# ViT tower on one NeuronCore: GpSimd adds the exponentials of attention 1's two key tiles, one row-sum product per head, one patch buffer, a new table of steps

## The reference

```
h = cat(cls, LN(LN(patches) @ W + b))
# attention 1
q, k, v = split((LN(h)) @ w_qkv.T)          # 12 heads x 64
q, k = q * rsqrt(norm(q over heads)), k * rsqrt(norm(k over heads))
h = h + softmax(q k^T / scale) v @ w_out.T + b_out
# attention 2
qkv = LN(h) @ Wqkv.T + bqkv + experts(LN(h)) # 12 heads x 16
h = h + softmax(q k^T / 4) v @ Wproj.T + bproj
```

## Time and profile before

| | |
|---|---|
| median of 3 runs | 3128.82 us (3126.43 to 3129.03) |
| profiled execution, its own time | 3129.87 us |
| its span, first to last instruction | 3128.1 us |
| mean granted TensorE clock | 0.984 |
| PE busy | 2969.7 us (95%), 41624 products |
| PEld busy | 2433.5 us (78%) |
| DVE busy | 2330.1 us (74%) |
| ACT busy | 1963.8 us (63%) |
| POOL busy | 594.8 us (19%) |
| DMA, mean over the span | 20 GB/s |

### The profile page before, as it was taken

The page is one execution under the profiler, slowest core; times in us unless marked ns, Lnnn a source line. Parts: engine busy times, 40 slices in busy tenths (PEclk is TensorE's granted clock), DMA queues, the critical chain, the costliest instruction groups (busy, mean ns, idle before and its releaser), DMA issues.

```text
span 3128.1 us, 98362 instructions
## 1 busy us (share of the span) xinstructions
PE 2969.7 (95%) x41624; PEld 2433.5 (78%) x41624; DVE 2330.1 (74%) x5441; ACT 1963.8 (63%) x3777; POOL 594.8 (19%) x859
## 2 busy tenths in 40 slices
PE   4799999999999999999999999999999999999996
PEld 3688788788788778778778778788788778778775
DVE  5677777777777777777777777777777777777773
ACT  2466666666666666666666666666666666666663
POOL 2121121121121121112112111111112112211210
PEclk7899999999999999999999999999999999999998
DMA  4000000000000000000000000000000000000000
GB/s 115 9 21 12 22 19 14 21 15 18 22 16 18 22 14 19 22 13 20 22 13 20 22 13 21 21 12 21 22 12 21 21 12 21 22 12 21 14 4 7
DMA packets 28389, 61.28 MB, mean 20 GB/s; under 512 B 4210, under 2 KB 18389, under 8 KB 27958
## 3 DMA queue, kind: packets, MB, share of 16 engines
q1 hardware_dynamic: 27958, 54.98, 6.0%
HBM read 45.29 MB, written 9.68 MB: 18 GB/s over the span
## 4 chain that ended last, share of the span: by engine, by line
PE 59%; DVE 35%; ACT 3%; issue 3%; DMA 0%; SPq 0%; POOL 0%; DVEq 0%; ACTq 0%
PE psum L676 9%; DVE mx L1090 8%; PE psum L685 8%; PE psum L585 8%; PE psum L602 8%; PE psum L664 4%; PE psum L712 4%; PE psum L612 3%; PE psum L646 3%; DVE st L989 3%; DVE mx L1105 2%; PE psum L715 2%; DVE qk L1184 2%; PE psum L722 2%; DVE o_t L1201 2%
## 5 line engine op out<-in xcount | busy, mean ns | idle before, releaser
L838 ACT ACTIVATE ebufs<-psum 99x788 f32<-99x788 f32 x768 | 592.0, 824 | 58.7 <-PE psum L664 45.4
L513 POOL TENSOR_TENSOR veps<-mv,eps_ln 99x2 f32<-99x2 f32 x256 | 116.0, 453 | 2273.6 <-DVE mv L1019 1341.1
L1105 DVE TENSOR_REDUCE mx<-psum 99x4 f32<-99x788 f32 x384 | 357.5, 973 | 137.6 <-PE psum L629 137.3
L1090 DVE TENSOR_REDUCE mx<-psum 99x4 f32<-99x788 f32 x384 | 362.9, 974 | 52.0 <-PE psum L621 52.0
L602 PE MATMUL psum<-hn_s,qk_w 128*128 128x197 f16 x3840 | 357.3, 250 | 13.9 <-DVE hn_s L1059 7.0
L602 PEld LDWEIGHTS psum<-hn_s,qk_w 128*128 128x128 f16 x3840 | 324.8, 98 | 35.2 <-DVE qk L1184 19.0
L676 PE MATMUL psum<-ebufs,vx 98*32 98x197 f32 (+1 forms) x6144 | 293.7, 331 | 0.0
L585 PE MATMUL psum<-emb_w,xb 128*99 128x193 f32 x1536 | 264.2, 328 | 0.7 <-DVE emb_b L901 0.7
L685 PE MATMUL psum<-out_w,qk 128*99 128x192 f32 x1536 | 263.8, 329 | 0.1
L585 PEld LDWEIGHTS psum<-emb_w,xb 128*99 128x99 f32 x1536 | 248.9, 166 | 2.4 <-DVE emb_b L901 1.0
L676 PEld LDWEIGHTS psum<-ebufs,vx 98*32 98x32 f32 (+1 forms) x6144 | 201.4, 110 | 57.1
(11 more groups left out here) (168 smaller groups left out, 6455.4 us busy)
## 6 DMA issues: line engine op xcount, KB each, us to landing
xb<-x_t SPq DMA_DIRECT2D x64, 591.0 KB, 3.8
out<-h SPq DMA_DIRECT2D x128, 73.5 KB
out<-h SPq DMA_DIRECT2D x64, 0.8 KB
vx<-w_qk SPq DMA_DIRECT2D x2, 384.0 KB, 10.7
...
```

Of the source, the lines that this page charges most:

```text
L838: nc.scalar.activation(ebuf[n].rearrange("p e a t -> p e (a t)"), psum[0:TR, b + 2 * half:b + 2 * half + 2, 0:2 * NT], ACT.Exp).then_inc(r ...
L1090: nc.vector.tensor_reduce(mx[s][:, :, 2 * i:2 * i + 2].rearrange("p a e -> p e a"), psum[0:TR, b:b + 2, 0:2 * NT].rearrange("p e (a t) -> ...
L1105: nc.vector.tensor_reduce(mx2[s][:, :, at:at + 2].rearrange("p a e -> p e a"), psum[0:TR, b + 2 * half:b + 2 * half + 2, 0:2 * NT].rearran ...
```

## The change

1. For each `ST` step POOL adds the exponentials of the two key tiles (99 partitions, 2 heads x 197 values) into one of three buffers `esum`. An `esum` buffer is free again when the sums of the `PV` that read it are made.
2. In `PV` the sums are one product per head over 99 rows of `esum`, no longer two over `ebufs`: 4 matrix products for 8. They stand between the two halves of the values (order of `c`: 0, 2, 1) and wait for POOL's add of `ST.2i+1`.
3. So that key row 98 counts once, the exponential of tile 0's row 98 is made zero: a constant of -30000 is set in the table of maxima and selected by `head_sel0` for that row. The `ST` products are as many as before. Some setup instructions are added.
4. `xb` is one buffer for two. The patches of the next image are loaded after `EMB` of this one.
5. `ORDER` is another table.

```
-        xb = two("xb", [128, KC, NT])
+        xb = sb("xb", [128, KC, NT])
...
+        ESUMS = 3
+        esum = [sb(f"esum{i}", [TR, 2, NT]) for i in range(ESUMS)]
...
+        st_order = steps["made_ST"]
+        esum_users = [st_order[n::ESUMS] for n in range(ESUMS)]
+
+        def sums_used(p):
+            return sums_made, ("PV", p[1], p[2] // 2)
...
-                    if kind == "QK" and i == 0 and now.which in ("first", "middle"):
+                    if kind == "EMB":
 
                         wait(sp, now, pe_sig["EMB"], ("EMB", s, 0))
-                        wait(sp, now, xsq_ready, ("X", s, 0))
-                        load(now.it + 1, s)
+                        n = now.image((kind, s, i)) + s
+                        if n < ITERS:
+                            load(n, 1 - s)
...
+                    elif p[0] == "ST":
+                        wait(pool, now, rd_sig["ST"], p)
+                        n = st_order.index(p) % ESUMS
+                        wait_free(pool, now, esum_users[n], sums_used)
+                        e = exp_tile(p)
+                        nc.gpsimd.tensor_tensor(esum[n][:], e[:, :, 0, :], e[:, :, 1, :], ALU.add
+                                                ).then_inc(tiles_added[1], 1)
...
-                                                      head_sel[r, 2 * i + e, :], neg_t[s][r, 0:NT],
+                                                      (head_sel if t else head_sel0)[r, 2 * i + e, :], neg_t[s][r, 0:NT],
...
-                        for c in (2, 0, 1):
+                        for c in (0, 2, 1):
+                            if c == 2:
+                                wait(pe, now, tiles_added, ("ST", s, 2 * i + 1))
+                                for j in range(4):
+                                    es = esum[st_order.index(("ST", s, 2 * i + j // 2)) % ESUMS]
+                                    mm = nc.tensor.matmul(ps(p, slice(32 * j, 32 * j + 32), slice(0, NT), 1),
+                                                          ones_col[:], es[:, j % 2, :], start=True, stop=True)
+                                mm.then_inc(sums_made[1], 1)
+                                continue
```

More of the change, by code:

```diff
@@ L51 @@
 ORDER = """
[L52 to L55, removed]
++X QK.0@4 -SM.4@6 =GB -SM.5@2 QK.1@0 QK.2@4 =T3@6 S +EMB@7 =QK2.0@6 =QK2.1@2 -NT@1 PS@3 =SM2.0@4
+-ST.0@0 V.0@2 =V2@4 =SM2.1@0 -ST.1@6 -ST.2@4 -ST.3@6 N.0 =SM2.2@0 -PV.0@4 -M.0 -ST.4@6 -ST.5@2 N.1
+=NT2@4 -PV.1@0 -PV.2@2 -M.1 -M.2 N.2 =ST2.0@4 +LA N.3 -OP@2 =ST2.1@4 SM.0@0 =PV2.0@5 -LD =ST2.2@0
+=M2.0 =PV2.1@6 +LB -T2@7 V.1@4 =M2.1 =PV2.2@2 +LC -G@7 =M2.2 SM.1@4 +T1@3 SM.2@0 SM.3@6 =OP2@2
 """
@@ L83 @@
 EBUFS = 4
+KEY_OUT = -30000.0
 def banks(p):
@@ L219, in vit_tower @@
         neg_t = two("neg_t", [128, NTP], F16)
-        head_sel = sb("head_sel", [128, H, TR], F16)
+        head_sel, head_sel0 = sb("head_sel", [128, H, TR], F16), sb("head_sel0", [128, H, TR], F16)
         qk2 = sb("qk2", [128, 2, 4 + 2 * G2, NTP], F16)
@@ L321, in vit_tower @@
         rinv_ready = signal("rinv_ready", ("PV",))
+        tiles_added = signal("tiles_added", ("ST",))
         sums2_ready = signal("sums2_ready", ("PV2",))
@@ L347, in reader, with release @@
             return rd_sig[p[0]], ({"PV": "M", "PV2": "M2"}.get(p[0], p[0]), *p[1:])
+        def release(q, freed, earlier):
+            sig, r = freed
+            assert earlier or POS[r] >= POS[q]
+            return sig, r, earlier and POS[r] >= POS[q]
         def wait_free(eng, now, order, freed):
             q, earlier = now.previous(order, now.at)
-            wait(eng, now, *freed(q), earlier)
+            wait(eng, now, *release(q, freed(q), earlier))
         def passes(eng, body):
@@ L423, in load @@
             def load(n, s):
[L424 removed]
+                sp.dma_start(xb[:], x_t[bass.ds(n * 2 + s, 1)].rearrange("b p c t -> (b p) c t")
                              ).then_inc(x_loaded[s], 16)
@@ L445, in _ @@
             load_group(v_loads, v_loaded)
-            load(0, 1)
             load_group(loads, consts_loaded)
@@ L578, in body @@
                     freed = [(b, *now.previous(users[b], p)) for b in banks(p)]
-                    for sig, q, earlier in dict.fromkeys((*reader(q, b), earlier) for b, q, earlier in freed):
+                    for sig, q, earlier in dict.fromkeys(release(q, reader(q, b), earlier) for b, q, earlier in freed):
                         wait(pe, now, sig, q, earlier)
@@ L673, in body @@
                                     eb = exp_tile(("ST", s, 2 * i + j // 2))
-                                    left = (vx[s][0:n, t, 4 * i + j, 32 * c:32 * c + 32] if c < 2
-                                            else ones_col[0:n])
                                     mm = nc.tensor.matmul(
-                                        ps(p, slice(32 * j, 32 * j + 32), slice(NT * (c % 2), NT * (c % 2) + NT), c // 2),
-                                        left, eb[0:n, j % 2, t, :], start=(t == 0), stop=(t == 1))
-                            if c == 2:
-                                mm.then_inc(sums_made[1], 1)
+                                        ps(p, slice(32 * j, 32 * j + 32), slice(NT * c, NT * c + NT)),
+                                        vx[s][0:n, t, 4 * i + j, 32 * c:32 * c + 32], eb[0:n, j % 2, t, :],
+                                        start=(t == 0), stop=(t == 1))
                     elif kind == "OP":
@@ L772, in body @@
                         wait_free(act, now, sq_users, squares_used)
-                        nc.scalar.activation(xsq, xb[s][:], ACT.Square).then_inc(xsq_ready[1], 1)
+                        nc.scalar.activation(xsq, xb[:], ACT.Square).then_inc(xsq_ready[1], 1)
                     elif kind in ("T1", "T2"):
@@ L944, in weights_of_scores @@
                 nc.vector.reciprocal(inv_scale[:], scale_sb[:])
+                for s in range(2):
+                    nc.vector.memset(neg[s][:].rearrange("p a (c k) -> p a c k", c=2)[:, :, :, H:H + 1], KEY_OUT)
+                nc.vector.tensor_copy(head_sel0[:], sel_raw.broadcast_to([128, H, TR])).then_inc(setup_w, 1)
+                splits[0] += 1
+                dve.wait_ge(setup_w, splits[0])
+                for e in range(2):
+                    nc.vector.tensor_tensor(head_sel0[:, :, TO:TR], head_sel0[:, :, TO:TR],
+                                            ident[:, 64 * e + H:64 * e + H + 1].unsqueeze(1).broadcast_to([128, H, 1]),
+                                            ALU.add).then_inc(setup_w, 1)
+                    splits[0] += 1
+                    dve.wait_ge(setup_w, splits[0])
                 nc.vector.tensor_copy(head_sel[:], sel_raw.broadcast_to([128, H, TR])
```

2 lines of the change are left out of this document (1 added, 1 removed).

## The result

The change makes the kernel slower by 0.8%: **3153.65 us** (median of 4 runs, 3148.92 to 3156.97), before 3128.08 (4 runs beside it, 3126.43 to 3129.03), ratio 1.0079 [1.0067, 1.0092]. The profiled execution took 3148.92 us with a span of 3147.1. The forecast was 3114 and faster; 3153.65 lies inside the range of 3062 to 3160, on the wrong side of no change. An execution that took over 1.5% longer than the fastest of its kernel, at a lower granted clock, is left out of every median here; there is one, in the run with `V.1` moved.

A forecast was written before the change was run, and what follows sets the result against it. PE (95% busy) was taken as the bound; per half pass 47.00 - 1.3 work + (2.9 - 1.85) waits = 46.76 us, over 64 half passes 15 us less, so 3114 us, range 3062 to 3160.

The forecast's parts named there:

- Work, 1.3 less, 43.85: PE's work per half pass: 1.05 us less for sum products, about 0.3 less for shape changes, leaving 43.85 us.
- `ST.3` 0.46: PE waits 0.46 us per half pass at `ST.3`, until the exponentials of `ST.1` free its banks.
- `PV2.0` 0.65: PE waits 0.65 us per half pass at `PV2.0` for bank 5, read with the lower half of `ST2.1`.
- `OP` (0.25): PE waits 0.25 us per half pass at `OP`, on `M.2`; held less sure, within 0.3.
- These four are less sure: PE's waits per half pass at `G` 0.35, `OP` 0.25, `OP2` 0.15, `QK.2` 0.15 us, each within 0.3.
- whoever is first holds the other off: DVE/POOL SBUF port: POOL's add of `ST.1` starts first and keeps DVE's `N.0` off for 0.9 us.
- `ST.5` 0.55: PE waits 0.55 us per half pass at `ST.5` for the maxima of `SM2.2`, late behind `N.0`; bounds 0 and 0.9.
- `PV.2` 0.35: PE waits 0.35 us per half pass before `PV.2`'s sums for POOL's add of `ST.5`, taken as 1.03 us.
- At nothing: Terms priced at zero: the six POOL adds' own time, one patch buffer, setup additions (once, about 2 us at most).
- rivals, 3: More small waits, at `X` before `QK.0` and at `G`: +0.4 us per half pass, 3140 us; chance 0.17.
- Rival 1: Saving kept: no port wait at `ST.5`, `OP` and `OP2` waits gone; 0.55 to 0.95 less, say 3075 us; chance 0.30.
- Rival 2: DVE's `N.1` beats the add of `ST.5`, PE waits 1.8 us before `PV.2`'s sums: +1.2, 3190 us; chance 0.13.

## Why the prediction was wrong

By its own steps, per half pass:

- *Work, 1.3 less, 43.85.* Right. The sum products of `PV.1` take half their time, and the shape changes are as counted, to that accuracy; 47.26 less the eight waits named below, 3.3 by the starts of loads, gives 43.9. Read by the starts of products a wait differs by up to 0.08, so all these numbers are good to about 0.1.
- *`ST.3` 0.46, `PV2.0` 0.65.* Right: 0.48 and 0.69. Both were worked out from a product's start, the exponential and the bank's release. `OP` (0.25) measured 0.28, but in part by luck: the table alone has 0.08 there, and the other 0.2 come from `N.1`, stretched by 0.38 beside the add of `ST.5`, a cost that the walk had not priced.
- *"These four are less sure", and what had no line.* **This is the step that failed; here the sign was lost.** `G` 0.35 measured 0.54, `OP2` 0.15 measured 0.28, `QK.2` 0.15 measured 0.33, and `SM2.0` was not in the walk at all and waits 0.26 for ACT's last cast of `QK2.1` (line 903). Together 0.76, 49 us. The run with the table alone shows it free of any port: forecast 46.85, measured 47.59 (`OP` waits only 0.08 there where the forecast had 0.25, so some 0.1 of its 0.74 stays unexplained). These are waits read from traces. Only that of `QK.2` was taken away by itself, and it gave back 0.07 of its 0.33, since the next ones grew; what the other three would give back is not shown.
- *The port, "whoever is first holds the other off": `ST.5` 0.55.* The mechanism is right, the winner was wrong. The walk had POOL ahead by 0.1, the trace by 0.08, and at that distance DVE wins. Instead of 0.55 at `ST.5` there were 0.48 at `PV.0`. That one loss took the other's place, so that the sum moved by less than 0.1, is luck. The run with `N.0` later put the wait where the prediction had it, with 0.41.
- *`PV.2` 0.35 behind the add of `ST.5`.* The add takes 0.89, not 1.03, and there is no wait at the sums. The walk had PE reach them 2.15 after the start of `PV.1`, and left out `PV.1`'s own sum products (0.33); measured it is 2.37, and the add has ended at 2.28. What this add did cost is the 0.2 at `OP`, through `N.1`, and four buffers took it away.
- *At nothing:* patch buffer and setup. Right, measured by themselves. Start and end were taken as unchanged; they are 3 us longer.

The sum then reads 46.76 + 0.76 - 0.35 (`PV.2`) + (0.48 - 0.55) + 0.09 (`ST.3`, `PV2.0`, `OP`) = 47.19. Measured are 47.26; the 0.07 between them are within what the readings can tell.

Of the rivals, 3 came nearest (more small waits, 3140), with a chance of 0.17. It named `X` and `G`, which are 0.37 of the 0.76, and 3153.65 lies in its range of 3130 to 3160. Rival 1 (the saving is kept) had 0.30, too much: with the port's loss cured, in the run with `N.0` early, the half pass is 46.79, with four buffers 46.64, and not the 45.8 to 46.2 that it named. Rival 2 had DVE winning, at `N.1`; it won at `N.0` instead, where the price is 0.48 and not 1.2.

Why the expectation for the table alone was 3160 to 3180 and right, while the forecast was not: it was written after the waits had been read.
